# Attention kernel on one core: the two scores in a row directly behind the value products, and the product with the inverse sums behind pair 5

## What is computed

```python
attn = jnp.einsum('bhqd,bhkd->bhqk', q, k) * scale
attn = jax.nn.softmax(attn, axis=-1)
out = jnp.einsum('bhqk,bhkd->bhqd', attn, v)
```

## Time and profile before

| | us |
|---|---|
| median of 3 runs | 4842.98 |
| lowest and highest | 4840.53, 4843.48 |
| the profiled execution, its own time | 4836.55 |
| its span in the profile | 4834.7 |
| TensorE busy | 4691.4 (97%) |
| GpSimd busy | 3223.0 (67%) |
| VectorE busy | 3170.4 (66%) |
| ScalarE busy | 2398.9 (50%) |

### The profile page before, as it was taken

One profiled execution on the slowest core, in us unless ns is written; L12 is line 12 of the kernel. 1 busy time (PEld: TensorE's weight loads), 2 busy tenths in 40 slices (PEclk: granted clock), 3 DMA queues, 4 the chain that ended last, 5 costly groups with the idle time before them and its releaser, 6 DMA issues. The chain is left out here.

```text
span 4834.7 us, 66456 instructions
## 1 busy us (share of the span) xinstructions
PE 4691.4 (97%) x24396; PEld 2773.0 (57%) x24396; DVE 3170.4 (66%) x5296; ACT 2398.9 (50%) x4653; POOL 3223.0 (67%) x1117
## 2 busy tenths in 40 slices
PE   8999999999899999999999999999999999999979
PEld 6887878878654444444444444444444444444447
DVE  4223232333188888888888888888888888888534
ACT  2111121121146666666666666666666666666621
POOL 1121212121249998989989989999899998998920
PEclk9999999999979999999999999999999999999989
DMA  5344343343346655656656566665665656655466
GB/s 172 103 127 122 109 138 102 119 129 111 91 106 130 137 127 125 138 125 137 133 124 139 124 131 136 126 139 120 132 137 124 140 125 132 137 124 121 90 225 236
DMA packets 254215, 633.49 MB, mean 131 GB/s; under 512 B 45252, under 2 KB 79044, under 8 KB 212936
## 3 DMA queue, kind: packets, MB, share of 16 engines
q0 software_dynamic: 36864, 268.45, 27.8%
q1 hardware_dynamic: 217032, 360.85, 27.0%
HBM read 224.96 MB, written 134.74 MB: 74 GB/s over the span
## 5 line engine op out<-in xcount | busy, mean ns | idle before, releaser
L927 DVE TENSOR_REDUCE unit_max<-mx_ps 128x1 f32<-128x512 f32 x4096 | 2535.2, 681 | 317.0 <-PE mx_ps L1002 310.9
L836 POOL TENSOR_TENSOR p_pair<-p_sb 128x2048 f32<-128x2048 f32 x512 | 2439.8, 4811 | 185.3 <-PE mx_ps L1026 128.3
L913 ACT ACTIVATE p_sb<-st_ps 128x512 f32<-128x512 f32 x4096 | 2061.9, 628 | 905.5 <-PE st_ps L1073 905.5
L1002 PE MATMUL mx_ps<-k_x,q_x 96*128 96x512 f32 x4096 | 1684.9, 415 | 21.5 <-DMA k_x<-k_lo_d 19.6
L1073 PE MATMUL st_ps<-q_x,k_x 97*128 97x512 f32 x4096 | 1607.8, 413 | 37.9 <-ACT p_sb L913 37.3
L1073 PEld LDWEIGHTS st_ps<-q_x,k_x 97*128 97x128 f32 x4096 | 770.3, 188 | 599.3 <-ACT p_sb L913 512.8
L1002 PEld LDWEIGHTS mx_ps<-k_x,q_x 96*128 96x128 f32 x4096 | 784.6, 192 | 456.7 <-DVE unit_max L927 234.3
L1014 PE MATMUL o_ps<-p_sb,v_sb 128*32 128x512 f32 x8192 | 986.8, 599 | 0.0
L285 POOL TENSOR_TENSOR h_lo<-h_f,h_hi 128x512 fp32r<-128x512 f32 x128 | 165.2, 1291 | 687.7 <-DVE h_hi L469 687.7
L1014 PEld LDWEIGHTS o_ps<-p_sb,v_sb 128*32 128x32 f32 x8192 | 214.0, 109 | 494.1 <-ACT p_sb L913 309.8
L469 DVE CAST h_hi<-h_f 128x512 fp32r<-128x512 f32 x128 | 55.0, 431 | 541.9 <-ACT h_f L342 541.9
(11 more groups left out here) (94 smaller groups left out, 3926.8 us busy)
## 6 DMA issues: line engine op xcount, KB each, us to landing
p_pair<-p_pair POOLq DMA_DIRECT2D x256, 1024.0 KB, 7.3
q_x<-q_hi_d SPq DMA_DIRECT2D x128, 256.0 KB, 8.6
k_x<-k_hi_d SPq DMA_DIRECT2D x68, 256.0 KB, 7.3
xt<-x SPq DMA_DIRECT2D x64, 256.0 KB, 2.7
stage<-w SPq DMA_DIRECT2D x32, 512.0 KB, 5.1
q_hi_d<-qk_hi SPq DMA_DIRECT2D x64, 256.0 KB, 3.0
q_lo_d<-qk_lo SPq DMA_DIRECT2D x64, 256.0 KB, 3.9
k_hi_d<-qk_hi SPq DMA_DIRECT2D x64, 256.0 KB, 2.6
```

Of the source, the lines that this page charges most:

```text
L836: pool.tensor_tensor(p_pair[:, slot, :, :], p_sb[:, n % SLOTS, :, :], p_sb[:, (n + 1) % SLOTS, :, :], ALU.add).then_inc(pair_done, 1)
L913: act.activation(p_sb[:, (L * G * KT + n) % SLOTS, h, :], st_ps[bank(g, m)][:, :], ACT.Exp, scale=SCALE).then_inc(exp_done, 1)
L927: dve.reduce_max(unit_max[:, n // 4, n % 4:n % 4 + 1], mx_ps[UNIT_PLACE[n] % RING][:, :], AX.X).then_inc(bank_read, 1)
L1002: pe.matmul(mx_ps[UNIT_PLACE[n] % RING][:, :], q_x[qc][0:R, h, t * P:(t + 1) * P], k_x[u][0:R, h, kc * 512:(kc + 1) * 512], start=True, st ...
```

## The change

The strings of `STEPS` get a new order behind V (and Z or T): `SSUSUUSUS` in place of `USSUSUSUS`. The number of letters stays. On GpSimd the call of `normalise`, with its two waits, moves from behind join 4 to behind pair 5, in front of the wait of pair 6.

```diff
-        STEPS = ["USUSUSUVUSSUSUSUS", "USUSUSUVUSSUSUSUS", "USUSUSUVZUSSUSUSUS", "USUSUSUVZUSSUSUSUS",
-                 "USUSUSUVUSSUSUSUS", "USUSUSUVUSSUSUSUS", "USUSUSUVTUSSUSUSUS", "USUSUSUVZUSSUSUSUS"]
+        STEPS = ["USUSUSUVSSUSUUSUS", "USUSUSUVSSUSUUSUS", "USUSUSUVZSSUSUUSUS", "USUSUSUVZSSUSUUSUS",
+                 "USUSUSUVSSUSUUSUS", "USUSUSUVSSUSUUSUS", "USUSUSUVTSSUSUUSUS", "USUSUSUVZSSUSUUSUS"]
@@
                     join(d, b)
                     pair(at, 5, c)
+                    if at > 0:
+                        normalise(at)
                     pool.wait_ge(sum_done, at * NS + 1)
                     pair(at, 6, a)
                     pool.wait_ge(pair_done, at * NA + 6)
                     pool.wait_ge(joined, (at * NJ + 3) * 16)
                     join(d, c)
-                    if at > 0:
-                        normalise(at)
                     pair(at, 7, b)
```

## The result

The changed kernel took 5095.84 us in the median (5090.45 to 5113.48) against 4843.23 before (four runs each): 1.0529 times as long, 95% interval 1.0503 to 1.0555. The profiled execution has a span of 5088.6 us. The forecast was slower, 4970 us; it came out slower by 252.6 us, twice the forecast 127, and 6 us above the range.

A forecast was written before the change was run, and what follows sets the result against it. TensorE's repeating group period of 50.62 us was taken as the bound, with GpSimd having some 2 us to spare. 49.5 + 2.7 + 0.5 = 52.7, +2.1 over some 62 groups, +130 us, gave 4970 us; range 4790 to 5090.

The forecast's parts named there:

- The swap: TensorE's steps: two score products first behind the value products would gain 0.04 us per step, 0.3 us per group.
- The copy of o: Step 0: with the product moved earlier, this copy no longer waits for GpSimd, gaining 0.79 us per group.
- TensorE's own period: TensorE's time per group if nothing else were late: 50.62 - 0.79 - 0.3 = 49.5 us.
- The first collision, join 4: Join 4, issued behind the key and query loads, lands late for step 2's sum product on TensorE: delay 2.7 us.
- The landing: Join 4's time from issue to landing behind the loads: taken as 10 us, between 7.3 (median) and 12.0 (one earlier row).
- even shares: DMA engines take turns between queues, so join 4 loses only what the loads have left, some 3 us: about 10.
- the earlier transfer first: DMA serves whichever transfer was issued ahead: join 4 would land in 9 us on average with loads nearly through.
- The second collision: The inverse loads fall right behind join 3's issue, delaying the product and making GpSimd's own loop about 52 us.
- From join 3 to the product: On GpSimd, time from join 3's issue to the product with the inverse sums: taken as 9 us, between 5.5 and 11.0.
- the sum, "49.5 + 2.7 + 0.5 = 52.7": TensorE's group period: 49.5 undisturbed, 2.7 for late join 4, 0.5 for the later product; +2.1 us per group.
- the worst case of the collisions (54.5): Both collisions in full: join 4 lands in 12, period 54 to 54.5 us, 5065 up to 5090 us; chance 0.17.

The follow-up runs named there:

- experiment 1: New strings of steps alone, the product with the inverse sums left behind join 4, against the kernel before: 4813.6 us, ratio 0.9945.
- both_sync: Also experiment 5, the repaired kernel: changed kernel with key, value, query loads waiting for join 4 and inverses written before the shift wait; 4759.4 us, 0.9833.
- experiment 3: Changed kernel, with SyncE's key, value and query loads waiting until join 4 of the group has landed: 4881.3 us, 1.0090 of the kernel before.
- experiment 10: Changed kernel, with the key, value and query loads waiting only for pair 7, not for join 4's landing: 4885.5 us, 1.0095 of the kernel before.
- experiment 12: As experiment 1, but the product with the inverse sums stands between pair 6 and join 4: 4831.6 us, 0.9977 of the kernel before.
- experiment 8: Changed kernel plus 16 additional identity products on TensorE before step 2's wait for join 4: 5063.0 us, 1.0462 of the kernel before.
- experiment 9: Changed kernel plus 8 additional identity products on TensorE before step 2's wait for join 4: 5051.6 us, 1.0441 of the kernel before.
- experiment 7: Changed kernel with write and loads of the inverse sums ahead of the shift wait, other loads not held back: 4894.0 us, 1.0111 of the kernel before.

## Why the prediction was wrong in size and right in kind

**The swap** was priced at 0.04 per step, 0.3 us per group, with 0.12 as the upper end. Measured 0.07 to 0.08 per step (5.83), 0.46 per group alone (50.65 - 50.19) and 0.7 in the repaired kernel. VectorE was hardly late. In the plain step at 2510.46 us of experiment 1 the fourth reduction ended 5.34 behind the start of the value products, where I had it (5.35), but the row-maximum product that waits for it started 0.12 later and the next value products 0.36 behind that, 5.82 in all. I had allowed 0.5 from the reduction to the end of that product.

**The copy of o** loses its wait for GpSimd, as forecast (in 37 of 44 groups): TensorE's own period without any other wait is 49.2 in both_sync; I had 49.5.

**The first collision, join 4** is the cause. TensorE's wait for it came where it was forecast and nearly as long (3.6 us in the mean of 43 groups; 2 to 4 forecast). That the join's landing decides most of it was shown from both sides: the same kernel with the loads out of its way is 210 to 215 us faster (experiments 3 and 10), and a kernel in which the product stands ahead of the join instead of behind it, so that the join's lead over the loads shrinks from 2.6 to 0.6 us, gets a landing of 11.8 instead of 7.6 (experiment 12). The landing was set at 10; it is 11.3, and 13 in the groups with the double key load. I argued that fewer loads are left ahead of it than in the earlier trace rows, and took less than the 12.0 of that row; the row was the better guide. The prediction weighed two readings, even shares (about 10) and the earlier transfer first (about 9), and the runs give neither: 11.3 with the loads 4 us ahead is more than both. They side with the earlier transfer in kind, since with the loads 2.6 us behind the join it is the loads that are late. Key loads of 256 KB landed in 7.3 us in the median before and in 4.3 after, the store in 6.7 and in 3.5.

**The second collision** was priced as if it set a floor of its own, near 52. It is real but conditional. The product comes behind its loads in the changed kernel (at T + 12.6, which I had as 13.0), but the floor of 50.4 and more that I still expected in experiment 5 isn't there: the inverse loads are ahead of join 3 in that kernel. From join 3 to the product I had 9; it was 10.4 in the changed kernel (12.6 - 2.2) and 8.0 in experiment 3. It costs 1.0 us per group where it is alone (experiment 3 against 1). That T + 12.6 came so near is in part luck: the inverse loads were issued 1.3 us earlier than in the old timing (T + 7.6 for 8.9), and took 5.0 instead of 3.3 us from the first issue until all four had landed, and the two nearly cancel.

**The step that failed** is the sum, "49.5 + 2.7 + 0.5 = 52.7": it has no term for TensorE's clock, and its term for join 4 (2.7, from a landing of 10) was too small. I costed a wait of TensorE by its length alone. From the start of step 2's sum product to the next T a group takes 23.3 us at full clock; in the changed kernel it is 24.1 in the mean of the 22 groups whose sum product ran at full clock (some of them slow down right behind it) and 26.1 in the 21 others, 25.1 in all. So 1.8 us per group from 2000 to 4400 are the slow clock's, and over all groups some 100 us of the 252.6. The sum by measured terms is 12.6 (T to the product) + 17.2 (to the sum product: 5.8 to the join's issue, 11.3 to its landing and 0.1) + 25.1 = 54.9, against 54.87 measured. My terms were 13.0, 15.8 and 23.9, 52.7 in sum. The landing brings 1.4 more, the clock 1.8; against that stand 0.4 for the earlier product and 0.6 because TensorE at full clock is faster than I had it. The Trainium skill (TensorE: Matmul & The Clock Gate, Part 1: The HAM clock gate) says that the array goes to half rate after it has stood idle, and the trace agrees: every wait over 4.1 us was followed by 0.50. I hadn't weighed it.

Taking the slow clock away by busy-work gave 33 and 44 us, not 100. Experiment 8 gives back 1.6 of the 1.8 us per group behind the sum product and loses 0.8 ahead of it; with 8 products (experiment 9) the stretch behind it is 24.1 and the sum product starts at T + 30.0. Of the 0.8, the additional products that are still running account for about 0.4. Why join 4 itself comes 0.3 to 0.4 us later was not tested and stays open.

**The range** ended at 5090 because I let the worst case of the collisions (54.5) stand for all that could go wrong; the true case had a landing of 11.3, between my 10 and the 12 of that case, and the clock on top.

## What to carry to other kernels

Moving a wait to an earlier place on an in-order engine is safe only if what it waits for is early too; here it pulled a critical DMA behind up to six uncritical loads. Two lines on another queue that hold those loads back turned a loss of 5.3% into one of 0.9%, and with the write of the inverses moved ahead as well it became a gain of 1.7%. Before such a move, list for every transfer behind it which other transfers it now trails, and price the landing by the row of the trace that has that order, not by the median. And a wait of TensorE of several microseconds is to be priced with the stretch at half clock behind it.

## What the runs showed of the hardware that I had not expected

An accumulating join of 1 MB landed in 7.0 to 7.6 us in the mean with loads queued 2.6 us or more behind it, and in 11.3 to 11.9 with 1.5 to 2.25 MB of loads queued 0.6 us behind or ahead of it: the lead that protects it lies between 1.2 us (a single join of experiment 7, which took 9.7) and 2.6 us. Beyond that edge the means of a kernel hardly differ between loads 0.6 us after the join and 4 us before it, but single joins do: in experiment 7 the ten that came 0.5 to 2.0 us behind the start of the loads, all with the double key load, took 14.1 to 15.9. Four loads of 64 KB issued beside a join took up to 4.2 us to issue in the changed kernel, and one of them up to 7.5 to land, against 1.7 and 2.0. TensorE's granted clock stood at 0.50 from 3082.2 to 3092.4 us in and behind a wait of 5.02 us, and was back at 1.00 just before the next value products (3092.49).
